# A graph network on one core: no clears between the indirect row transfers, each issued when the one before has landed

## The reference

```
h = jnp.maximum(_layernorm(x), 0.0)
# layer 0: per edge, R = relu(edge_weight @ w1 + b1) @ w2 + b2, spherical harmonics of edge_attr,
#          msg = contraction of R, the harmonics and h[src];  out.at[dst].add(msg)
x = x + _L0_gnn_ref(h, edge_weight, edge_attr_3, edge_index, ...)
h = jnp.maximum(_layernorm(x), 0.0)
# layers 1, 2, 3 (32 -> 128 -> 128 -> 32 features), self loops added, norm = deg^-1/2[src] * deg^-1/2[dst]
#          h = relu(segment_sum((h @ W)[src] * norm, dst) + b)
x = x + _L1_gnn_ref(h, edge_index, ...)
```

## Time and profile before

| what | value |
|---|---|
| median of 3 runs | 5768.08 us (5767.51 to 5774.85) |
| span of the profiled execution, first to last instruction | 5779.7 us |
| PE, DVE, ACT, POOL busy | 4258.6, 3608.0, 2702.7, 4889.1 us |
| indirect transfers (L782), POOL | 3616, 3636.6 us busy |
| clears (L762), POOL | 3616, 1234.8 us busy |
| mean granted clock of PE | 0.816 |

### The profile page before, as it was taken

One profiled execution on the slowest core, in us unless ns is written; L12 is line 12 of the kernel. 1 busy time (PEld: TensorE's weight loads), 2 busy tenths in 40 slices (PEclk: granted clock), 3 DMA queues, 4 the chain that ended last, 5 costly groups with the idle time before them and its releaser, 6 DMA issues.

```text
span 5779.7 us, 179150 instructions
## 1 busy us (share of the span) xinstructions
PE 4258.6 (74%) x62463; PEld 3147.7 (54%) x62464; DVE 3608.0 (62%) x8469; ACT 2702.7 (47%) x6550; POOL 4889.1 (85%) x7276
## 2 busy tenths in 40 slices
PE   5777777777777777755555555889898889766666
PEld 3444444444444444444444444778787778554554
DVE  8777777777777777776666666333333334555555
ACT  4444444444444444466666666344444444433333
POOL 7888888888888888768888888688888889588886
PEclk9999999999999999955555555899989999767767
DMA  3111111111111111333332332332333333444444
GB/s 87 33 33 33 33 33 31 33 33 33 33 33 32 32 33 33 36 71 77 77 77 77 77 77 71 114 90 85 91 91 85 91 91 100 119 119 126 122 127 107
DMA packets 494970, 400.88 MB, mean 69 GB/s; under 512 B 269575, under 2 KB 454828, under 8 KB 493537
## 3 DMA queue, kind: packets, MB, share of 16 engines
q10 hardware_dynamic: 146996, 207.67, 10.6%
q0 software_dynamic: 115712, 109.02, 10.3%
q1 hardware_dynamic: 231536, 74.48, 5.9%
HBM read 375.52 MB, written 15.29 MB: 68 GB/s over the span
## 4 chain that ended last, share of the span: by engine, by line
POOL 50%; issue 40%; PE 5%; POOLq 2%; DVE 2%; DMA 1%; ACT 0%; DVEq 0%; SPq 0%
POOL rows L782 29%; POOL pause L762 21%; POOLq L761 2%; PE radial L2067 2%; PE psX L2082 1%; PE psT L2082 1%; PE sums L2153 1%; PE radial L2209 0%; DMA table<-arena 0%; PE radial L2222 0%; DMA rows<-table,idx 0%; DMA xn<-in_x 0%; POOLq L760 0%; PE radial L2008 0%; DVE rows L1827 0%
## 5 line engine op out<-in xcount | busy, mean ns | idle before, releaser
L782 POOL DMA_INDIRECT rows<-table,idx x3616 | 3636.6, 1006 | 803.0 <-POOL pause L762 483.7
L762 POOL MEMSET pause<- 128x256 f32 x3616 | 1234.8, 341 | 2.5
L1942 PEld LDWEIGHTS sums<-scratch,onehot 128*64 128x64 f32 x9408 | 789.7, 144 | 465.0 <-DVE scratch L1377 228.6
L2067 PE MATMUL radial<-arena,shared 128*32 128x96 bf16 (+1 forms) x31200 | 926.4, 266 | 154.2 <-DVE shared L1613 75.1
L1942 PE MATMUL sums<-scratch,onehot 128*64 128x264 f32 (+1 forms) x9408 | 984.1, 356 | 32.6 <-DVE scratch L1377 26.2
L2067 PEld LDWEIGHTS radial<-arena,shared 128*32 128x32 bf16 (+1 forms) x31200 | 664.8, 116 | 294.4 <-issue 72.0
L2153 PE MATMUL sums<-onehot,rows 128*128 128x80 f32 (+1 forms) x2844 | 371.0, 298 | 576.7 <-DMA rows<-table,idx 571.8
L1007 ACT CAST scratch<-radial 128x480 bf16<-128x480 f32 x860 | 476.9, 555 | 665.7 <-PE radial L2067 657.6
L1360 DVE TENSOR_TENSOR scratch<-radial,shared 128x768 f32<-128x768 f32 x784 | 743.4, 948 | 0.0
L1927 PE MATMUL radial<-shared 64*128 64x384 f32 x3136 | 730.5, 546 | 0.0
L880 ACT COPY shared<-rows 128x192 f32<-128x192 f32 x196 | 89.4, 456 | 1264.1 <-DMA rows<-table,idx 1262.9
(11 more groups left out here) (237 smaller groups left out, 5969.3 us busy)
## 6 DMA issues: line engine op xcount, KB each, us to landing
scratch<-places_d ACTq DMA_DIRECT2D x242, 800.0 KB
rows<-table,idx POOLq DMA_INDIRECT x3616
shared<-in_edge_weight SPq DMA_DIRECT2D x390, 128.0 KB, 2.9
idx<-in_src SPq DMA_DIRECT2D x451, 4.0 KB
table<-arena SPq DMA_DIRECT2D x24, 256.0 KB, 2.8
table<-arena SPq DMA_DIRECT2D x2, 1176.0 KB, 10.6
accT<-in_edge_attr SPq DMA_DIRECT2D x2, 1152.0 KB
table<-arena SPq DMA_DIRECT2D x24, 96.0 KB, 2.0
```

The source lines that it names most:

```text
L762: nc.gpsimd.memset(pause[:, :], 0.0).then_inc(made, 1)
L782: (pool.indirect_dma_start(rows_3[:, r, j, :] if n in (1, 3) else rows[:, r, j, 0:WIDTH[n]], None, tables[n], bass.IndirectOffsetOnAxis(ap ...
L1942: last = nc.tensor.matmul(there, onehot[:, u % 2, 4 * h + t, 0:SW], taken_from, start=(h + q + part == 0), stop=(h == 1 and q == 1 and par ...
L2067: last = nc.tensor.matmul(d, from_src[n][:, h, i, t, :], table_of(n, s), start=True, stop=True, tile_position=(0, 32 * i))
```

## The change

The tile `pause`, its clear and the register `pauses` go. Ahead of each indirect transfer POOL now waits until the transfer before it has landed: for the tiles 1 to 7 of a group on the group's own semaphore, for tile 0 on that of the group before. In the loops the count stands in one register for each of the four semaphores.

```diff
-            pauses = pool.alloc_register("pauses")
-
-            def pause_between(step, n, u, j):
-
+            landed = [pool.alloc_register(f"landed{u}") for u in range(UNROLL)]
+
+            def after_landing(step, n, u, j):
+
+                r = (u if j else u - 1) % UNROLL
                 if step.peeled:
-                    before = TPG * (sum(GATHERED[:n]) + step.it * step.groups + u) + j
-                    if before:
-                        pool.wait_ge(made, 9 + before)
+                    landed_before = sum(GATHERED[:n]) + step.it * step.groups + u - (j == 0)
+                    if landed_before >= 0:
+                        pool.wait_ge(gathered[r], 16 * (landed_before // UNROLL * TPG + (j if j else TPG)))
                 else:
-                    pool.wait_ge(made, pool.snap(pauses))
-                    pool.reg_add(pauses, pauses, 1)
-                nc.gpsimd.memset(pause[:, :], 0.0).then_inc(made, 1)
+                    pool.wait_ge(gathered[r], pool.snap(landed[r]))
+                    pool.reg_add(landed[r], landed[r], 16)
...
                         for j in range(TPG):
                             col = j % 2 * KS + j // 2
+                            after_landing(step, n, u, j)
                             (pool.indirect_dma_start(rows_3[:, r, j, :] if n in (1, 3) else rows[:, r, j, 0:WIDTH[n]], None, tables[n],
                                                      bass.IndirectOffsetOnAxis(ap=idx[:, r, col:col + 1], axis=0))
                                  .then_inc(gathered[r], 16))
-                            pause_between(step, n, u, j)
...
-                pool.reg_mov(pauses, 9 + TPG * (sum(GATHERED[:n]) + LOOP[n][0]))
+                for u in range(UNROLL):
+                    pool.reg_mov(landed[u], 16 * TPG * ((sum(GATHERED[:n]) + LOOP[n][0]) // UNROLL) + (16 if u < UNROLL - 1 else 0))
```

More of the change, by code:

```diff
@@ L61 @@
 PAD_REL = -1000.0
-PAUSE = 256
 assert NG % UNROLL == 0 and PTAIL * KS == ETAIL and PTAIL <= P and NG == 2 * NB
@@ L295, in gnn_kernel @@
         one = sb("one", [P, 1])
-        pause = sb("pause", [P, PAUSE])
         flag = sb("flag", [P, 1])
```

## The result

The changed kernel takes 12,128.65 us (median of 4 runs, 12,120.20 to 12,133.46) against 5767.80 (median of 4): 2.103 times as long, 95% interval 2.0995 to 2.1054. The forecast was 11,970 us, range 9,900 to 12,900.

A forecast was written before the change was run, and what follows sets the result against it. POOL's chain of transfers was taken as the bound. Steps of landing, traffic and landing-to-start gave 4991, 2331, 2660 and 1713 us for layers 0 to 3; with 276 outside, 11,970 us, 80% range 9,900 to 12,900.

The forecast's parts named there:

- The landing: Start of a transfer to landing of its rows: 2.45 us without other traffic, 1.006 mean duration plus 1.44.
- My terms: Landing with traffic added to the quiet 2.45 us: 0.1 more in layer 1, 0.3 more in layers 2 and 3.
- The traffic of layers 1 to 3: Delay from ACT's loads of lists of places: 0.1 us a transfer in layer 1, 0.3 in layers 2 and 3.
- Landing to start in the loops: POOL's sequencer stands at the register add, then readies the transfer: 0.02 + 0.03 + 0.71 = 0.76 us a step.
- the 0.71 before the first transfer of layer 1: Gap from last register move to transfer start, read as the sequencer's time to get an indirect transfer going.
- Rival A: Sequencer's preparation is hidden while the wait is pending, so every step is landing + 0.10: 9,960 us; chance 12%.
- Outside the loops: The transfer itself can carry the wait: 0.10 us from landing to next start.
- 276: Time in us outside the layers' transfers (start, tables between layers, end), added to the sum of the steps.
- Cover: Other engines: PE, even at 20 us a group, stays below 26; SP's index loads stay hidden; costed at nothing in layers.
- Rival C: The waits are met early, only the clears go: step 1.17 us, DVE and PE holding layers 0 and 2; 4,870 us; 3%.

The follow-up runs named there:

- the written-out queue: The changed kernel with POOL's queue written out in full, waits of constant count instead of register counts in loops: 10,954.51 us, 1.895 times the kernel before.

## Why the prediction was right

*The bound and the mechanism.* As forecast, the wait turned a chain of 1.5 us steps, with the latency hidden, into one of landing plus what comes after it. Putting the wait into the kernel with its clears kept gives the whole loss; taking the wait out of the changed kernel gives 4,921 us.

*The landing.* 2.45 us was taken from the last transfers of three layers. Over all transfers it is 2.46, 2.62, 2.71 and 2.66 us in layers 0 to 3. My terms were 2.45, 2.55, 2.75 and 2.75. Two errors cancel in layer 0, and that is luck: seven transfers of eight take 2.36, and the first of each group 3.04, which I had not foreseen. The traffic of layers 1 to 3 was taken as 467 us; the lists cost some 336 by the count above.

*Landing to start in the loops.* 0.76 taken, 0.75 in the median and 0.78 in the mean. The single row that it rested on, the 0.71 before the first transfer of layer 1, was read rightly: 0.48 for the sequencer and 0.19 to the start, and the written-out queue shows that most of it goes when the transfer carries the wait. Rival A was right for a transfer that carries its wait and wrong for the loops. The Trainium skill, "Perfetto Trace Analysis", section "DMA Instruction — SWDGE (GPSIMD)", has the instruction decoded and queued before its semaphores are looked at: the trace agrees where the semaphore is the transfer's own, with 0.26 us, against 0.75 where an instruction ahead of it carries the wait.

*Outside the loops.* The term most mis-sized: 0.10 taken from the subtraction of L801, measured 0.26 in the median and 0.33 in the mean. That row was of a subtraction, and the first transfer of each group pays 0.76 outside the loops too. 576 x 0.23 = 132 us, most of the 160 us between the forecast and the result. The rest nearly cancels: landing to start in the loops 3040 x 0.023 = 70, the landings of layer 0 +11, of layer 1 +54, of layers 2 and 3 -79, and 245 us outside the layers' transfers against 276.

*Cover.* The other engines kept up. PE's granted clock fell in layer 0 from 0.92 to 0.70 and in layer 2 from 0.91 to 0.70; PE is then busy 1332 us for 787 / 8 = 98 groups in layer 2, 13.5 us each, below the 27 of a group. SP's index loads stayed hidden as a wait. The loads of edge weights that follow them in layer 0, which the prediction did not price, delay the transfer that they meet.

*Rival C.* Its price was 4,870 us; the kernel that realises it takes 4,921. Both of its terms were off: the step is 1.25 us and not 1.17, so it and not DVE sets layer 0; and layer 2 has 1040 / 791 = 1.315 us a transfer, not the 1.567 at which I had PE hold it. PE's work in layer 2 was 11.2 / 8 = 1.40 us a transfer before, so PE never held it at 1.567, and with the granted clock at 0.99 in place of 0.91 it is 1018 / 791 = 1.29. That the price came out 1% low is luck, as these errors go against each other.

## What to carry to other kernels

Here a row transfer kept its issuing engine busy for about 1 us (a step of 1.25), and its rows were there after about 2.4. Only the first counts while enough transfers are under way; a wait for a landing ahead of the next issue makes the second count. With two under way the step was still 1.7 to 2.0 us, and with four the loss was down to 151 us. Before putting such a wait in, find in the trace of before the last transfer of a stage: start to its reader's start, plus what comes between a landing and the next start, is the new step. Look also at which instruction carries the wait. Where it was the transfer, 0.26 us came between; where it was an instruction of the sequencer ahead of it, the add on a register in the loops or a wait of its own at the first transfer of a group, it was 0.75, 0.5 us more each time.

## What the runs showed of the hardware

A transfer behind another starts after a gap of 0.30 us, behind a clear of 16 columns after 0.12 of clear and 0.18 of gap, so a short instruction between two transfers was free in the median step. The mean duration of a transfer on POOL was 1006 ns with clears alone, 951 with waits alone, 962 with both and 968 with neither: 17% of the transfers took over 1.1 us in the first and 2 to 4% in the others; why is open. A wait for a landing cost 0.26 us from landing to start on the transfer itself and 0.75 on the sequencer instruction ahead of it. A transfer that met a load of 800 KB landed 0.8 to 1.6 us later than the others of its layer, one that met a load of a fifth of the bytes still 0.5 to 0.9 us, and one that met the two loads of edge weights, 128 KB each, 0.7 us.
